# A fused attention and feed-forward kernel: TensorE issues no filler products before the first turning of the input

## The reference, cut to what matters

```python
# x: (8, 256, 128) f32, 16 heads of 64, feed-forward width 512
xn = layernorm(x)                        # no scale, no shift
x2 = layernorm(xn) * ln_w + ln_b         # input of the attention
q, k, v = (einsum('bsd,hde->bshe', x2, W) + b for W, b in ...)
scores = where(causal, einsum('bqhe,bkhe->bhqk', q, k) / 8, -inf)
z = einsum('bhqk,bkhe->bqhe', softmax(scores), v)
attn = einsum('bqhe,hed->bqd', z, W_o) + b_o
Wq1, Wq2 = ternary(W1), ternary(W2)      # clip(round(W / (mean|W| + eps)), -1, 1)
ffn = relu(xn @ Wq1.T + b1) @ Wq2.T + b2
out = x + attn + ffn
```

## Time and profile before

| | us |
|---|---|
| median of 3 runs | 235.34 (234.69 to 235.57) |
| the profiled execution | 235.85 |
| its span, first to last instruction | 234.1 |
| busy in the span: PE | 226.2 (97%) |
| DVE | 201.0 (86%) |
| ACT | 195.4 (83%) |
| POOL | 183.6 (78%) |

### The profile page before, as it was taken

The page is one execution under the profiler, slowest core; times in us unless marked ns, Lnnn a source line. Parts: engine busy times, 40 slices in busy tenths (PEclk is TensorE's granted clock), DMA queues, the critical chain, the costliest instruction groups (busy, mean ns, idle before and its releaser), DMA issues.

```text
span 234.1 us, 7703 instructions
## 1 busy us (share of the span) xinstructions
PE 226.2 (97%) x2692; PEld 193.0 (82%) x2692; DVE 201.0 (86%) x776; ACT 195.4 (83%) x733; POOL 183.6 (78%) x363
## 2 busy tenths in 40 slices
PE   8999999999999999899999899999989999999995
PEld 8985878888888888798888798898879898779874
DVE  2209997999899989999999889999989899999961
ACT  1239999997799899988999699989999799998940
POOL 6308999999986997889789978899688879897900
PEclk9999999999999999999999999999999999999999
DMA  6960047564357467564557447654656356647820
GB/s 159 320 196 3 3 98 178 134 136 105 93 123 156 118 134 179 133 140 95 134 133 152 108 115 173 141 140 100 133 136 158 83 151 152 150 126 171 190 68 22
DMA packets 24022, 30.66 MB, mean 131 GB/s; under 512 B 2608, under 2 KB 23088, under 8 KB 23984
## 3 DMA queue, kind: packets, MB, share of 16 engines
q1 hardware_dynamic: 23840, 30.16, 54.6%
q10 hardware_dynamic: 144, 0.02, 0.0%
HBM read 4.73 MB, written 1.05 MB: 25 GB/s over the span
## 4 chain that ended last, share of the span: by engine, by line
PE 34%; POOL 23%; DVE 15%; ACT 13%; DMA 8%; SPq 3%; issue 2%; POOLq 0%; DVEq 0%
DMA pT<-blocks 8%; POOL prob L309 7%; POOL prob L308 5%; DVE s_ps L597 5%; PE s_ps L816 5%; PE m_ps L854 5%; PE s_ps L727 5%; ACT prob L485 4%; DVE blocks L610 4%; SPq L345 3%; ACT prob L487 3%; POOL xh_cur L407 3%; POOL xn_cur L388 3%; PE m_ps L858 2%; PE m_ps L781 2%
## 5 line engine op out<-in xcount | busy, mean ns | idle before, releaser
L485 ACT ACTIVATE prob<-s_ps,neg_max 128x256 f32<-128x256 f32 x128 | 69.5, 544 | 10.7 <-DVE neg_max L597 10.7
L597 DVE CUSTOM_DVE_ANT_0 s_ps<-s_ps,causal 128x256 f32<-128x256 f32 x128 | 54.5, 426 | 12.7 <-PE s_ps L816 12.6
L309 POOL TENSOR_SCALAR prob<-prob,inv_sum 128x256 f32<-128x256 f32 x126 | 62.2, 494 | 0.0
L308 POOL TENSOR_SCALAR prob<-prob,inv_sum 128x128 f32<-128x128 f32 x126 | 48.5, 385 | 14.5 <-DVE inv_sum L604 14.4
L610 DVE STREAM_TRANSPOSE blocks<-prob 128x768 f32<-128x768 f32 x62 | 58.7, 961 | 1.1 <-POOL prob L309 0.6
L487 ACT ACTIVATE prob<-s_ps,neg_max 128x128 f32<-128x128 f32 x128 | 55.7, 435 | 0.0
L816 PE MATMUL s_ps<-qk 64*64 64x64 f32 (+2 forms) x1280 | 46.7, 278 | 0.4 <-ACT prob L487 0.3
L816 PEld LDWEIGHTS s_ps<-qk 64*64 64x64 f32 x1280 | 39.0, 132 | 9.4 <-issue 4.3
L474 ACT ACTIVATE qk<-m_ps,vecs 128x256 f32<-128x256 f32 x64 | 35.1, 548 | 9.5 <-PE m_ps L777 8.3
L854 PE MATMUL m_ps<-pT,v 128*64 128x256 f32 x256 | 40.1, 389 | 2.8 <-DMA pT<-blocks 2.6
L597 DVE CUSTOM_DVE_ANT_0 s_ps<-s_ps,causal_first 128x128 f32<-128x128 f32 x128 | 42.2, 330 | 0.0
(11 more groups left out here) (124 smaller groups left out, 543.4 us busy)
## 6 DMA issues: line engine op xcount, KB each, us to landing
pT<-blocks SPq DMA_DIRECT2D x124, 192.0 KB, 3.6
xT_cur<-in_xT SPq DMA_DIRECT2D x8, 128.0 KB, 2.2
outT<-out_sb SPq DMA_DIRECT2D x8, 128.0 KB, 1.7
x_all<-in_x SPq DMA_DIRECT2D x1, 768.0 KB, 8.7
wv_raw<-in_w_v SPq DMA_DIRECT2D x2, 256.0 KB, 4.8
wo<-in_w_o SPq DMA_DIRECT2D x1, 512.0 KB, 6.8
x_all<-in_x SPq DMA_DIRECT2D x2, 128.0 KB, 3.8
wq_raw<-in_w_q SPq DMA_DIRECT2D x2, 128.0 KB, 2.4
```

Source lines behind the costliest of these rows:

```text
L308: op(first, first, inv_sum[:, j, 2 + h:3 + h], 0.0, ALU.mult, ALU.add)
L309: last = op(later, later, inv_sum[:, j, h:h + 1], 0.0, ALU.mult, ALU.add)
L485: nc.scalar.activation(later, s_ps[:, pair % 2, h, 0:S].rearrange("p (g j k) -> p g j k", g=TILES, j=QT), ACT.Exp, bias=neg_max[:, j, h:h ...
L597: last = nc.vector.tensor_tensor_reduce(out=sc, in0=sc, in1=mask, scale=-SCALE, scalar=-MASKED, op0=ALU.add, op1=ALU.min, accum_out=neg_ma ...
```

## The change

Both counts of `BUSY` become 0, and the word `wk3:0` leaves `PE_HEAD`. So TensorE issues none of its filler products: 20 ahead of the first turning, 6 behind it, 3 between `s5` and `s6`. The bank of `wk3` passes directly from `v3` to `pr0` of batch 1. The tile `ones` becomes 256 instead of 128 columns wide, and DVE sets all of it. The helper `stay_busy`, which is no longer called with a count above 0, would use all 256 columns.

```diff
-BUSY = (20, 6)
+BUSY = (0, 0)
 PE_HEAD = ("xb:0 pr0:0 pr1:3 xn:2 s0 s1 v0:3 pr2:1 pr3:2 v1:3 s2 v2:1 s3 pr4:3 ta:0 pr5:2 pr6:1 s4 pr7:3 v3:0 "
-           "xh+:1 f0:2 s5 wk3:0 s6 pr0+:0 bo:2 f1:1 pr1+:3 s7 xn+:0 z0:1 s0+ pr2+:3 pr3+:2 pr4+:0 s1+ pr5+:1 "
-           "z1:3 s2+ z2:2 s3+ pr6+:0 oa:3 f0+:1 s4+ z3:0 s5+ v0+:1 v1+:2 pr7+:0 ob v2+:1 v3+:2 xh++:3 f1+:0 s6+ "
-           "s7+ z0+:1 pr0++:0 pr1++:2 pr2++:3 xn++:0 pr3++:1 s0++")
+           "xh+:1 f0:2 s5 s6 pr0+:0 bo:2 f1:1 pr1+:3 s7 xn+:0 z0:1 s0+ pr2+:3 pr3+:2 pr4+:0 s1+ pr5+:1 z1:3 s2+ "
+           "z2:2 s3+ pr6+:0 oa:3 f0+:1 s4+ z3:0 s5+ v0+:1 v1+:2 pr7+:0 ob v2+:1 v3+:2 xh++:3 f1+:0 s6+ s7+ z0+:1 "
+           "pr0++:0 pr1++:2 pr2++:3 xn++:0 pr3++:1 s0++")
 PE_PLAN = ("z1-:2 s1 pr4:3 v0:0 pr5:2 v1:1 pr6:3 s2 s3 oa-:2 f0:3 z2-:1 z3-:0 s4 s5 pr7:1 v2:3 ob- v3:3 xh+:0 "
...
-        ones = sb("ones", [P, P])
+        ones = sb("ones", [P, S])
...
-                    nc.tensor.matmul(into, ones[:, :], ones[:, 0:E], start=True, stop=True)
-
-            stay_busy(BUSY[0], s_ps[:, 1, 1, 0:E])
+                    nc.tensor.matmul(into, ones[:, 0:P], ones[:, :], start=True, stop=True)
+
+            stay_busy(BUSY[0], s_ps[:, 1, 1, 0:S])
...
-                nc.tensor.matmul(bank("ta", 0, 0)[:, 0:2], ones[:, :], abs_sum[:, :], start=True, stop=True).then_inc(abs_total, 1)
+                nc.tensor.matmul(bank("ta", 0, 0)[:, 0:2], ones[:, 0:P], abs_sum[:, :], start=True, stop=True).then_inc(abs_total, 1)
...
-                    stay_busy(BUSY[1], s_ps[:, 1, 1, 0:E])
+                    stay_busy(BUSY[1], s_ps[:, 1, 1, 0:S])
...
-                    stay_busy(index, bank(kind, index, b)[:, 0:E])
+                    stay_busy(index, bank(kind, index, b)[:, 0:S])
```

## The result

The changed kernel takes 229.13 us (median of 4 runs, 229.00 to 229.67) against 235.27 (4 runs, 234.69 to 235.57). The ratio is 0.9746, with a 95% interval of 0.9721 to 0.9771: 6.1 us less. The forecast was 230.4, with 229.0 to 232.2 as its range. The profiled execution took 229.0 us, with a span of 227.2 against 234.1.

What follows compares the result with a forecast made beforehand. Fixed filler on TensorE ahead of the first projections was taken to bound the head, no single engine the whole. 235.85 (profiled) - 5.4 + 0.4 (clock) = 230.85; forecast median 230.4 us, range 229.0 to 232.2.

Steps and rivals of the forecast that it cites:

- The input's path: Head, from `xh_cur` through the turning and `x2T` to the first projection: without filler, projections start 5.4 us earlier.
- POOL beside DVE: Head, POOL's `xn_cur` now running beside DVE's `x2T`: if both slow each other down, at most some tenths of a us.
- The loads have margin: Input loads for q, k and v behind the head: least margin on later loads some 2 us, none takes the wait over.
- The clock: TensorE's rise from 1.2 to 2.4 GHz in the head: +0.4 us taken, with -1.8 and +4.8 as bounds.
- The rule on the clock: Skill's warm-up advice for TensorE: filler should have brought upper-level projections, some 1.8 us lost by removal; trace showed no such reward.
- `wk3` and the memset at 0: Fillers before `s6` and DVE's wider `ones`: 0 taken for both; `wk3` could gain 0.3 us at most.
- Rival B's variant: Unprofiled runs before had the clock's rise ahead of the projections, so the change gives up 1.8 us: 231.7.
- A: Rival, head: the clock rises earlier than before, down to -1.8 us, 228.1 to 229.3; chance 0.08.
- B: Rival, head: filler partly held the clock up; rise late, at 15 to 20 us, 231.8 to 234.3; chance 0.09.
- C: Rival, further on: loads, or POOL and regrouping DMAs, take back 1 to 3 us, 231 to 233; chance 0.05.
- D: Rival, from 11.3 us on: clock does not rise in the head, slower than before; 238.3 if at 28 us; chance 0.03.
- E: Rival, head: the filler was hidden anyway, so no gain, 235.3; chance 0.01.

Runs made afterwards that it cites:

- idle-time kernel: Kernel before with both filler counts 0 and TensorE made to wait for the second half of v before the first projection: 235.49 us, ratio 0.997.
- twice the filler: Kernel before with 40 instead of 20 fillers of 64 columns ahead of the turning: 242.5 us, one execution.
- wide and too long: Changed kernel with 15 fillers of 256 columns ahead of the turning and 6 behind it: 233.14 us, ratio 0.9889.
- version with fitting filler of 256 columns: Changed kernel with 5 fillers of 256 columns ahead of the turning and 1 behind it: 226.59 us, ratio 0.967; once more 228.14 us, ratio 0.9712.
- second series: Changed kernel, unaltered, measured again in six runs against the kernel before: 229.36 us, ratio 0.976.
- four series without filler at the start: Changed kernel twice (ratios 0.9746, 0.976), and kernel before with both counts 0 but `wk3` and narrow `ones` kept, twice (0.9808, 0.9783).

## Why the prediction was right, and where its sizes were off

- **The fixed filler was the bound of the head.** Right. The idle-time kernel and the changed kernel show it from both sides: nearly the same delay without filler, the same time as before (ratio 0.9932 to 1.0008); no delay, 5.4 to 6.1 us less.
- **The input's path.** I had `x2T` at 6.40 and the first projection streaming at 7.33; DVE began at 6.26, and the projection's record is at 6.90 against 12.51. The shift of this step is 5.6, not 5.4 us. Most of the difference stands ahead of `x2T`: TensorE took up the first half of `xh_cur` at 5.48, before DVE had ended the second (5.58), and ended the turning at 6.14, where I had 6.27.
- **POOL beside DVE.** I allowed some tenths. `xn_cur` took 2.33 us instead of 1.58, so 0.75, and ended at 8.60. It took 1.58 in all three traces in which the projections start late behind filler (before, twice the filler, wide and too long) and 2.33 to 2.58 in the eleven in which DVE starts on `x2T` between 6.0 and 6.4. It is needed at 10.45 here, so the cover held. In the version with fitting filler of 256 columns it took 2.47 us from 6.24 and ended at 8.71, and its turning stands at 8.76, behind a gap: there it binds already.
- **The loads have margin.** Right: in the waiting list of the first 40 us no engine waits for a load but DVE for x and ACT for the first weights, as before.
- **The clock.** I took +0.4 us, with -1.8 and +4.8 as the ends. Counted from the first projection's record, the first trace after has the rise 0.4 us sooner than before (3.6 against 4.0), the second 2.0 us later (12.9 - 6.9 = 6.0), and the division moved by 5.67 and 4.64 us. Against the 5.6 us of the projections' start the term is thus -0.1 and +1.0. My value lies between; what I lacked is that it is not one number. That it lies between is partly luck, since the prediction gave no reason for a spread within one program.
- **The rule on the clock.** In all 14 traces the first TensorE records are at the lower level, and the upper one comes during work of TensorE. But not all work brought it. After 92 records of 64 columns over 20 us the level was still the lower one. Where 10 records of 256 or 18 of 128 stood ahead of the turning, it was the upper one before the first projection in three traces of four; in one of these three it had not yet risen at the turning (two transposes in 0.64 us), and came with the two records behind it. The Trainium skill says that "the default state is throttled, and activity releases the throttle" ("TensorE: Matmul & The Clock Gate", "What's actually happening"). This case agrees with the sentence, but not with the prediction's reading of it, that the filler of 64 columns should have been rewarded. The price, halved projections for 1.8 us, was right: 1.79 us between the first projection and the turning of `xn_cur`, from before to the wide filler that is too long.
- **`wk3` and the memset at 0.** Right by the traces: 0.2 us, given back; the memset took 0.27 us in place of 0.17 and ended 2 us before DVE's next work.
- **The sum.** 230.85 for the profiled execution against 229.0. Of the 1.85 us, about 0.2 is the shift, 0.5 the clock's term (+0.4 forecast, -0.1 measured), and 1.2 the rest behind the division, which the prediction treated as fixed and which isn't. The median of 229.13 lies only 0.1 us above the lower end of the range. With the 1.2 us of unexplained rest it took luck to stay inside; the second series, 5.4 us less where 4.9 were forecast, is the fairer measure.
- **Rivals.** Rival B's variant (before had its rise ahead of the projections in unprofiled runs) has nothing for it: the idle-time kernel, whose TensorE stood still for 5.70 us ahead of its projections, takes the same time over ten runs (235.49 against 235.69), where the variant would have had it some 1.1 us slower (1.8 for the clock, 0.7 less delay). A did not come. B did not come in its size, a rise at 15 to 20 us; the second trace's 12.9 is a step towards it. C, D and E did not come.

## What to carry to other kernels

Filler products ahead of a wait are a fixed delay once they outlast it: read when the awaited input was ready (here 5.6 us) beside when TensorE took it up (9.6). Before counting on filler for the clock, look in the trace at whether its own records get shorter; if they don't, more of the same only delays. Filler of 128 or 256 columns that ended when the input came gave the fastest versions here (ratios of 0.966 to 0.971 to the kernel before, against 0.975 to 0.981 in the four series without filler at the start). It did not in every execution: one of the four traces had the rise only at 10.5.

## What the runs showed of the hardware

- The granted clock of the trace reads 1.00 in stretches where every load takes 333 ns and later ones of the same shape 192 (kernel before). At the start of a span the durations have to be read, not that column.
- For the same dense projections from 6.9 us on, the rise to the upper level came between 10.5 and about 12.9 us. Between two traces of the changed kernel that alone moves the first division from 15.03 to 16.06.
- The two POOL instructions of `xn_cur` took 1.58 us together before and 2.33 when DVE worked beside them on the first `x2T` and the low parts of the weights. In the changed kernel the first of the two kept its 0.80 us and the second, most of it beside the low parts, took 1.54. In twice the filler and in the wide filler that is too long, where DVE stood idle then, the pair again took 1.58.
- The waits for one kind of regrouping DMA add up to anything from 0.6 to 3.2 us in the 14 traces, of 11 kernels, and the part behind the division moves by 2.3 us, roughly with them. Within one kernel that was traced twice they moved by 0.1 to 0.7 us.
